# Graph attention, two graphs at a time: scores and contexts in one stretch, one transpose for both

## The chip, the cores and the metric

One core of a Trainium2 chip runs the whole program; there is one launch. The metric is the time of one execution in microseconds. Engines: TensorE (PE, with PEld for its weight loads), VectorE (DVE), ScalarE (ACT), GpSimd (POOL) and SyncE (SP), which issues the DMAs.

## The reference

For each of 128 graphs with 128 nodes and 384 features: layer norm, relu, attention with 6 heads of 64 masked by the graph's adjacency matrix, an output projection, and the input added back.

```python
h = jnp.maximum(_layernorm(x, axis=-1), 0.0)
q = _heads(h @ Wq + bq); k = _heads(h @ Wk + bk); v = _heads(h @ Wv + bv)
scores = jnp.einsum('bhqd,bhkd->bhqk', q, k) / np.sqrt(HEAD_SIZE)
probs = jax.nn.softmax(scores + jnp.where(adj, 0.0, NEG)[:, None], axis=-1)
ctx = jnp.einsum('bhqk,bhkd->bhqd', probs, v)      # heads side by side: 384
return x + ctx @ Wf + bf
```

Inputs: x (128, 128, 384) and four 384 x 384 weights with biases in float32, adj (128, 128, 128) bool. Everything is computed to about float32 accuracy.

## The kernel before

A float32 matmul is replaced by three float16 ones: each operand is split into an upper part (a rounded copy, made by ScalarE) and a lower part (the rest, made by VectorE or GpSimd), and `split_product` adds upper x upper, upper x lower and lower x upper in PSUM, nine matmuls per product.

The work is a software pipeline in slots of one graph. `slots` runs each engine's `slot(t, k)`: written out for the first slots, then in a loop of eight slots, then written out again. Each engine executes its list in the order in which `slot` calls its parts, and the semaphores (`wait`) tie the lists together. Nothing else sets the order. In slot t:

- SyncE loads x of graph t + 11, transposes h of graph t + 8 by DMA (`turn_h`), stores the output of graph t - 3 and transposes the probabilities of graph t - 1 by DMA (L285).
- GpSimd makes 1/std and the shift of graph t + 9 (`factors`, four small instructions), the mask of graph t + 1, the lower half of h (L795), x plus the output bias of graph t + 4 (L807) and normalises graph t's probabilities in two halves of three heads (L816).
- ScalarE rounds the probabilities of graph t - 1 (L494), applies the norm (L505) and rounds h (L515) of graph t + 9, takes six exponentials of graph t (L473), and rounds Q/K tiles, v and the context.
- VectorE adds the mask to the scores (L650, two instructions), takes maxima (L664), makes the lower probabilities of graph t - 1 (L699), statistics of graph t + 10, the residual of graph t - 3 (L615), reciprocals, and the lower halves of Q/K, context and v.
- TensorE: scores of graph t (`scores`), output projection of graph t - 3, a Q/K tile for a group of four graphs (512 columns; six tiles in four slots, so every other slot has two), the context of graph t - 2 (`context`), the v projection of graph t + 4.

`scores` and `context` are 18 small matmuls each, in pairs that use half of the array. Scores (ps_s) take two PSUM banks, Q/K two, the context (ps_c) and the output projection (ps_r) one each, v (ps_v) two: eight in all.

Of the kernel before, what the change touches and what calls it, by code (L numbers as in the profile page):

```python
# [6 lines left out]
F16 = mybir.dt.float16  # L7
# [12 lines left out]
TILES = 2 * PAIRS  # L20
RING = 2 * GROUP
# [4 lines left out]
LOAD, STATS, NORM, TURN, LATE = 11, 10, 9, 8, 3  # L26
XB = 4
# [3 lines left out]
FIRST, LOOP_END = 4, GRAPHS - 12  # L31


def graph_attention(nc, x, adj, Wq, bq, Wk, bk, Wv, bv, Wf, bf, out):
    ctx = ExitStack()
    with ctx:
# [8 lines left out]

# [24 lines left out]
        x_in = sb("x_in", [128, RING, FEAT])  # L70
        x_bias = sb("x_bias", [128, RING, FEAT])
        adj_in = sb("adj_in", [128, 2, GROUP, NODES], U8)
        mask = sb("mask", [128, 2, NODES])
        stats = sb("stats", [128, 2, 6])
        moments = sb("moments", [128, 2, 2])
        rstd = sb("rstd", [128, 2, 2])
        shift = sb("shift", [128, 2, 2])
        h = sb("h", [128, 2, FEAT])
        h_parts = sb("h_parts", [128, 2, 2, FEAT], F16)
        ht = sb("ht", [128, 2, 2 * KT, COLS], F16)  # L80

# [4 lines left out]
        v_hi = sb("v_hi", [128, 2, GROUP, FEAT], F16)  # L86
        v_lo = sb("v_lo", [128, 2, GROUP, FEAT], F16)
# [4 lines left out]
        parts = sb("parts", [128, 2, 2, HEADS * NODES], F16)  # L92
        pt = sb("pt", [128, 2, 2 * HEADS, NODES], F16)
        ct_hi = sb("ct_hi", [128, PAIRS, NODES], F16)
        ct_lo = sb("ct_lo", [128, PAIRS, NODES], F16)
# [27 lines left out]
        x_loaded = [sem(f"x_loaded{r}") for r in range(RING)]  # L123
        adj_loaded = [sem(f"adj_loaded{p}") for p in range(2)]
# [14 lines left out]
        mask_step = sem("mask_step")  # L139
# [18 lines left out]
        def valid(u):  # L158

            return not isinstance(u, int) or 0 <= u < GRAPHS  # L160

        def wait(eng, semaphore, value):

            if not isinstance(value, int) or value > 0:
                eng.wait_ge(semaphore, value)  # L165

        def slots(eng, slot, weights=lambda t: None):


# [3 lines left out]
            with eng.Fori(FIRST, LOOP_END - RING + 1, RING) as base:  # L173
                for i in range(RING):
                    slot(base + i, FIRST + i)
            for t in range(LOOP_END, GRAPHS + LATE):
                slot(t, t % RING)

        def turns(u, k, d):

            r = (k + d) % RING
            return 2 * (u - r) + 16

        def group_of(t, k):

            return (k % RING) // GROUP, k % GROUP

# [3 lines left out]
        PROJECTED = [[0, 1], [2], [3, 4], [5]]  # L191
        COUNT = [1, 1, 2, 1, 1, 2]

        def tile_count(t, j, tile):

            slot = next(i for i in range(GROUP) if tile in PROJECTED[i])
            return 2 * (t + GROUP) + 2 * (slot - j) + (1 if PROJECTED[slot][-1] != tile else 2)

        PAIR_COUNT = [2, 5, 8]
# [7 lines left out]

        @block.sync
        def _(sp):
# [3 lines left out]
            def weights(t):  # L213

                column = lambda b: b.rearrange("(k p) -> p k", p=128)
                if t == 1 - LOAD:
                    with nc.allow_non_contiguous_dma(reason="a bias vector, once"):
                        sp.dma_start(bv_col[:, :], column(bv)).then_inc(bv_loaded, 16)
                    load_weight("f", Wf)
                if t == 2 - LOAD:  # L220
                    load_weight("q", Wq)
                if t == 3 - LOAD:
                    load_weight("v", Wv)
                if t == 4 - LOAD:
                    load_x(3)
                    load_weight("k", Wk)
                    with nc.allow_non_contiguous_dma(reason="bias vectors, once"):
# [4 lines left out]
                    for u in range(4, RING):  # L232
                        load_x(u)
# [617 lines left out]
```

## Time and profile before

| | |
|---|---|
| median of 3 runs | 1001.98 us (1000.74 to 1003.02) |
| profiled execution, its own time | 1000.85 us |
| its span in the profile | 999.0 us |
| busy: TensorE | 948.1 us (95%) |
| busy: VectorE | 838.4 us (84%) |
| busy: ScalarE | 780.8 us (78%) |
| busy: GpSimd | 670.3 us (67%) |
| granted TensorE clock, mean | 0.991; 0.77 in the last 24 us |
| DMA | 130.86 MB, 60.4% of 16 engines |

Matmuls overlap, so TensorE's busy time is the union of overlapping spans; what a block of matmuls costs is read from the starts of successive blocks. On VectorE and ScalarE too, an instruction starts a little before the one ahead ends, if it waits for nothing. The profile's chain of waits that ended last runs mostly over GpSimd (41%) and issue (44%); it follows one of several nearly equal chains.

### The profile page before, as it was taken

The page shows a single profiled execution, that of the slowest core. Times are in us where ns is not written, and L with a number is a line of the kernel's source. Part 1 is how long each engine was busy: PE and PEld are TensorE (multiplying, and loading weights), DVE is VectorE, ACT ScalarE, POOL GpSimd, SP SyncE. Part 2 cuts the span into 40 slices and gives each one's busy share as a digit, 9 for nine tenths or more (in the row PEclk, how much of TensorE's full clock was granted, in tenths as well). Part 3 has the DMA queues.
Part 4 walks back from the last instruction along what each step waited for, and adds up shares of the span by engine and source line. Part 5 has one row for each costly group of instructions (what it writes and reads, how often), then busy time and mean ns, then how long its engine had stood idle before and what let it go on. Part 6 is the DMA issues. An engine that isn't in the chain of part 4 may idle for free.

```text
span 999.0 us, 28223 instructions
## 1 busy us (share of the span) xinstructions
PE 948.1 (95%) x8649; PEld 510.8 (51%) x8649; DVE 838.4 (84%) x1621; ACT 780.8 (78%) x2373; POOL 670.3 (67%) x1163
## 2 busy tenths in 40 slices
PE   1889999999999999999999999999999999999976
PEld 0445555555555555555555555555555555555543
DVE  4688888888888888898888888888889888888774
ACT  3687788888878888888888887888888888888663
POOL 4676677777776767767777677776776777777431
PEclk9999999999999999999999999999999999999997
DMA  7447656566566565655656656656565565666454
GB/s 199 75 90 152 123 126 141 127 139 147 130 135 136 129 140 130 148 133 126 141 127 141 145 130 133 138 129 139 132 148 133 124 143 128 140 146 121 92 94 90
DMA packets 359834, 130.86 MB, mean 131 GB/s; under 512 B 325376, under 2 KB 359808, under 8 KB 359808
## 3 DMA queue, kind: packets, MB, share of 16 engines
q1 hardware_dynamic: 359808, 130.54, 60.4%
q8 instruction: 13, 0.21, 0.1%
q14 instruction: 13, 0.11, 0.0%
HBM read 29.82 MB, written 25.17 MB: 55 GB/s over the span
## 4 chain that ended last, share of the span: by engine, by line
issue 44%; POOL 41%; PE 5%; ACT 2%; POOLq 2%; DVE 2%; DMA 2%; SPq 0%; DVEq 0%; ACTq 0%
POOL x_bias L807 13%; POOL s L816 11%; POOL rstd L775 7%; POOL mask L786 3%; POOL shift L778 2%; POOL rstd L770 2%; PE ps_qk L301 2%; POOL shift L772 2%; DMA pt<-parts 2%; POOL h_parts L795 1%; POOLq L165 1%; PE ps_v L301 1%; PE ps_r L301 1%; ACT s L473 1%; DVE s L650 1%
## 5 line engine op out<-in xcount | busy, mean ns | idle before, releaser
L473 ACT ACTIVATE s<-s,neg_max 128x128 f32<-128x128 f32 x768 | 297.7, 390 | 53.3 <-DVE neg_max L664 53.3
L816 POOL TENSOR_TENSOR s<-s,inv_sums 128x384 f32<-128x384 f32 x256 | 212.2, 829 | 132.7 <-DVE inv_sums L639 132.7
L795 POOL TENSOR_TENSOR h_parts<-h,h_parts 128x384 f16<-128x384 f32 x128 | 121.3, 948 | 146.1 <-ACT h_parts L515 146.1
L301 PE MATMUL ps_v<-w_hi_v,ht 128*128 128x384 f16 x768 | 209.4, 328 | 0.0
L301 PE MATMUL ps_qk<-ht,w_hi_q 128*128 128x512 f16 x576 | 172.5, 381 | 3.6 <-DVE w_lo_q L545 3.3
L301 PE MATMUL ps_qk<-ht,w_hi_k 128*128 128x512 f16 x576 | 171.3, 379 | 0.0
L807 POOL TENSOR_TENSOR x_bias<-x_in,out_bias 128x384 f32<-128x384 f32 x128 | 170.1, 1329 | 0.4
L494 ACT ACTIVATE parts<-s 128x768 f16<-128x768 f32 x128 | 107.3, 838 | 55.0 <-POOL s L816 55.0
L650 DVE SCALAR_TENSOR_TENSOR s<-ps_s,unscale,mask 128x384 f32<-128x384 f32 x256 | 145.2, 609 | 1.0
L473 ACT ACTIVATION_READ_ACCUMULATOR s<-s,neg_max 128x1 f32 x768 | 145.5, 189 | 0.0
L301 PE MATMUL ps_r<-w_hi_f,ct_hi 128*128 128x384 f16 x384 | 128.2, 334 | 14.3 <-DVE ct_lo L688 13.1
L699 DVE TENSOR_TENSOR parts<-s,parts 128x768 f16<-128x768 f32 x128 | 136.9, 1070 | 1.9 <-ACT parts L494 1.9
L664 DVE TENSOR_REDUCE neg_max<-s 128x6 f32<-128x768 f32 x128 | 122.0, 953 | 9.3
L301 PE MATMUL ps_r<-w_lo_f,ct_hi 128*128 128x384 f16 x384 | 127.0, 331 | 0.0
L301 PE MATMUL ps_r<-w_hi_f,ct_lo 128*128 128x384 f16 x384 | 126.8, 330 | 0.0
L301 PE MATMUL ps_v<-w_lo_v,ht 128*128 128x384 f16 x384 | 125.2, 326 | 0.0
L505 ACT ACTIVATE h<-x_in,shift,rstd 128x384 f32<-128x384 f32 x128 | 90.4, 706 | 42.1 <-POOL shift L778 39.9
L301 PE MATMUL ps_qk<-ht,w_lo_q 128*128 128x512 f16 x288 | 109.7, 381 | 0.0
L301 PE MATMUL ps_qk<-ht,w_lo_k 128*128 128x512 f16 x288 | 109.2, 379 | 0.0
L627 DVE SCALAR_TENSOR_TENSOR k_lo<-ps_qk,qk_bias,k_hi 128x512 f16<-128x512 f32 x96 | 71.2, 741 | 45.3 <-ACT k_hi L453 45.2
L301 PEld LDWEIGHTS ps_v<-w_hi_v,ht 128*128 128x128 f16 x768 | 74.8, 97 | 53.3
L405 PEld LDWEIGHTS ps_c<-pt,v_hi 128*64 128x64 f16 x1536 | 68.5, 110 | 64.6 <-issue 44.2
(77 smaller groups left out, 1806.6 us busy)
## 6 DMA issues: line engine op xcount, KB each, us to landing
x_in<-in_x SPq DMA_DIRECT2D x128, 192.0 KB, 2.9
out<-y SPq DMA_DIRECT2D x128, 192.0 KB, 2.1
ht<-h_parts SPq DMA_TRANSPOSE x128, 2.9
adj_in<-in_adj SPq DMA_DIRECT2D x32, 64.0 KB, 2.7
pt<-parts SPq DMA_TRANSPOSE x128, 3.7
w_raw_f<-in_L_gnn_Wf SPq DMA_DIRECT2D x1, 576.0 KB, 5.2
w_raw_q<-in_L_gnn_Wq SPq DMA_DIRECT2D x1, 576.0 KB, 6.2
w_raw_v<-in_L_gnn_Wv SPq DMA_DIRECT2D x1, 576.0 KB, 7.3
```

What stands on the lines that cost most here:

```text
L301: last = mm(psum, parts_a[a](i), parts_b[b](i), start=n == 0, stop=n == len(todo) - 1)
L473: last = activation(s[:, b, hd, :], s[:, b, hd, :], ACT.Exp, bias=neg_max[:, b, hd:hd + 1], accum_out=sums[:, b, hd:hd + 1])
L494: activation(parts[:, b, 0, :], s[:, b, :, :].rearrange("p h n -> p (h n)"), ACT.Copy).then_inc(parts_hi, 1)
L505: activation(h[:, r % 2, :], x_in[:, r, :], ACT.Relu, bias=shift[:, r % 2, 1:2], scale=rstd[:, r % 2, 1:2]).then_inc(h_ready, 1)
L627: nc.vector.scalar_tensor_tensor(out=lower, in0=ps_qk[tile % 2][:, :], scalar=qk_bias[:, which, pair:pair + 1], in1=upper, op0=ALU.add, op ...
L650: nc.vector.scalar_tensor_tensor(out=s[:, b, odd * PAIRS:(odd + 1) * PAIRS, :], in0=ps_s[:, odd, 0:PAIRS * NODES].rearrange("p (h n) -> p ...
L664: nc.vector.tensor_reduce(neg_max[:, b, :], s[:, b, :, :], AX.X, ALU.max, negate=True).then_inc(max_ready, 1)
L699: tt(parts[:, b, 1, :], s[:, b, :, :].rearrange("p h n -> p (h n)"), parts[:, b, 0, :], ALU.subtract).then_inc(parts_lo, 1)
L775: nc.gpsimd.tensor_tensor(rstd[:, b, 1:2], rstd[:, b, 0:1], minus_half[:, :], ALU.pow).then_inc(rstd_step, 1)
L795: nc.gpsimd.tensor_tensor(h_parts[:, b, 1, :], h[:, b, :], h_parts[:, b, 0, :], ALU.subtract).then_inc(h_lo_ready, 1)
L807: nc.gpsimd.tensor_tensor(x_bias[:, r, :], x_in[:, r, :], out_bias[:, :], ALU.add).then_inc(xb_ready, 1)
L816: nc.gpsimd.tensor_tensor(s[:, b, half, :], s[:, b, half, :], inv_sums[:, b, half].unsqueeze(2).to_broadcast([128, PAIRS, NODES]), ALU.mul ...
```

## The change

The slot becomes two graphs (a duo). There are 64 duos, pipeline distances count in duos, and the loop runs four slots per turn.

- TensorE (one slot): Q/K tile, Q/K tile, output projection of the first graph of duo t - 3, v of the first graph of duo t + 1, Q/K tile, v of the second, output projection of the second, scores of both graphs of duo t, contexts of both graphs of duo t - 2. Three Q/K tiles a slot, made two duos ahead.
- PSUM: ps_s takes four banks (two per graph). Contexts, v and output projections share the two banks of ps_m.
- `parts`, `pt`, `ct_hi`, `ct_lo` hold both graphs; `parts` and `pt` have two buffers of a duo. One DMA transpose turns the probabilities of a duo, another its h.
- s has one buffer for each graph of a duo. Masked scores are one instruction per graph (768 columns), normalising is one, reciprocals are one, lower context is one for both graphs, h is rounded for both graphs at once (768 columns), and so is its lower half and the bias addition.
- x is loaded a second time into x_res for the residual; the bias is added there in place.
- The weights are loaded in another order and prepared in other slots.

```diff
+DUOS = GRAPHS // 2
+RING = 4
...
-LOAD, STATS, NORM, TURN, LATE = 11, 10, 9, 8, 3
-XB = 4
+LOAD, STATS, NORM, TURN, AHEAD, VALUES = 7, 6, 5, 4, 2, 1
+CONTEXT, LATE = 2, 3
...
-        ps_s = ps("ps_s", [128, 2, 512])
+        ps_s = ps("ps_s", [128, 2, 2, 512])
         ps_qk = [ps(f"ps_qk{i}", [128, COLS]) for i in range(2)]
-        ps_c = ps("ps_c", [128, 512])
-        ps_r = ps("ps_r", [128, 512])
-        ps_v = [ps(f"ps_v{i}", [128, 512]) for i in range(2)]
+        ps_m = ps("ps_m", [128, 2, 512])
...
+                if valid(t):
+                    if not static or t >= FIRST:
+                        wait(sp, parts_lo, 2 * t - 2)
+                    sp.dma_start(x_res[:, k, :, :], x_rows[:, bass.ds(2 * t, 2), :]).then_inc(xr_loaded[k], 16)
...
+                if valid(t - 2):
...
+                    sp.dma_start_transpose(pt[:, k % 2, :, :, :].rearrange("p g a n -> p (g a) n"),
...
+                    for i in range(2):
+                        wait(sp, y_ready, 2 * u + 1 + i)
...
+                    else:
+                        wait(pe, y_ready, 2 * (t - LATE) + 1)
+                    at = slice(i * NODES, (i + 1) * NODES)
+                    split_product(ps_m[:, i, 0:FEAT],
...
+                    elif valid(t + VALUES):
+                        wait(pe, v_ready, 2 * (t + VALUES) + 1)
+                    split_product(ps_m[:, 1 - i, 0:FEAT], [lambda n: ct_hi[:, i, n, :], lambda n: ct_lo[:, i, n, :]],
...
                     wait(pe, turned[ku % 2], 8 * (u - ku % 2) + 16)
-                    wait(pe, v_ready, u + 1)
-                    wait(pe, ct_lo_ready, u)
+                    if i == 1:
+                        if valid(t + VALUES):
+                            wait(pe, v_ready, 2 * (t + VALUES) + 2)
...
+                    else:
+                        wait(pe, y_ready, 2 * (t - LATE) + 2)
...
-                scores(t, k)
-                projection(t - 3)
-                qk_tile(tiles[0])
-                context(t - 2, k - 2)
-                v_tile()
-                if two:
-                    qk_tile(tiles[1])
+                                last = mm(ps_m[rows, i, at], a[:, ku, i, f:f + HEAD],
+                                          pt[:, ku % 2, i, b + odd * PAIRS + pair, :], start=n == 0, stop=n == 2)
+                    if i == 0:
+                        last.then_inc(ct_ps, 1)
+                qk_tile(0)
+                qk_tile(1)
+                projection(0)
+                values(0)
+                qk_tile(2)
+                values(1)
+                projection(1)
+                scores(0)
+                scores(1)
+                context(1)
+                context(0)
...
-                if isinstance(t, int) and t < -GROUP:
-                    norm()
-                    upper_h()
-                else:
-                    upper_probs()
-                    norm()
-                    upper_h()
-                    exponentials(0)
-                    qk_tile(tiles[0])
-                    context()
-                    exponentials(1)
...
+                upper_context()
+                norm(0)
+                qk_upper(0)
+                upper_probs(1)
+                exponentials(0, 0)
+                qk_upper(1)
+                exponentials(0, 1)
+                v_upper(0)
+                exponentials(1, 0)
+                qk_upper(2)
+                v_upper(1)
+                upper_probs(0)
+                norm(1)
+                exponentials(1, 1)
+                upper_h()
...
+                    wait(dve, scores_ps, 2 * u + 1 + i)
+                    wait(dve, mask_ready, u + 1)
+                    wait(dve, parts_lo, 2 * u - 1 + i)
+                    nc.vector.scalar_tensor_tensor(
+                        out=s[:, i, :, :], in0=ps_s[:, i, :, 0:PAIRS * NODES], scalar=unscale[:, 0:1],
+                        in1=mask[:, i:i + 1, :].to_broadcast([128, HEADS, NODES]),
+                        op0=ALU.mult, op1=ALU.add).then_inc(masked, 1)
...
+                def lower_probs(i):
+                    u, b = t - (1, 2)[i], (k - (1, 2)[i]) % 2
+                    if not valid(u):
+                        return
+                    wait(dve, parts_hi, 2 * u + 1 + i)
+                    tt(parts[:, b, i, 1, :], s[:, i, :, :].rearrange("p h n -> p (h n)"), parts[:, b, i, 0, :],
                        ALU.subtract).then_inc(parts_lo, 1)
...
+                masked_scores(0)
+                lower_context()
+                maxima(0)
+                qk_lower(0)
+                lower_probs(1)
+                masked_scores(1)
+                maxima(1)
+                residual(0)
+                qk_lower(1)
+                spread()
+                lower_v(0)
+                spread_done()
+                reciprocals(0)
+                mean_and_variance()
+                qk_lower(2)
+                lower_v(1)
+                residual(1)
+                lower_probs(0)
+                reciprocals(1)
...
-                    wait(pool, h_ready, u + 1)
-                    wait(pool, y_ready, u - RING + 1)
-                    nc.gpsimd.tensor_tensor(x_bias[:, r, :], x_in[:, r, :], out_bias[:, :], ALU.add
+                    wait(pool, xr_loaded[r], 4 * (u - r) + 16)
+                    nc.gpsimd.tensor_tensor(x_res[:, r, :, :], x_res[:, r, :, :],
+                                            out_bias[:, :].unsqueeze(1).to_broadcast([128, 2, FEAT]), ALU.add
                                             ).then_inc(xb_ready, 1)
...
+                    wait(pool, inv_ready, 2 * u + 1 + i)
+                    nc.gpsimd.tensor_tensor(s[:, i, :, :], s[:, i, :, :],
+                                            inv_sums[:, i, :].unsqueeze(2).to_broadcast([128, HEADS, NODES]),
...
-                mask_of_next()
+                normalised(1)
                 lower_h()
                 biased_x()
+                wait_for_mask()
                 normalised(0)
-                normalised(1)
+                mask_of()
```

The order of instructions on GpSimd, in one place of the written-out start. s is the probabilities, x_res or x_bias is x plus the output bias, h_parts is the lower half of h. Before, the slots of two graphs:

```order
L770 TENSOR_TENSOR rstd<-moments,eps 128x1
L772 TENSOR_TENSOR shift<-moments,minus_one 128x1
L775 TENSOR_TENSOR rstd<-rstd,minus_half 128x1
L778 TENSOR_TENSOR shift<-shift,rstd 128x1
L786 TENSOR_SCALAR mask<-adj_in 128x128
L795 TENSOR_TENSOR h_parts<-h,h_parts 128x384
L807 TENSOR_TENSOR x_bias<-x_in,out_bias 128x384
L816 TENSOR_TENSOR s<-s,inv_sums 128x384 x2
```

That is one slot, and the next repeats it. After the change, one slot of two graphs:

```order
L722 TENSOR_TENSOR rstd<-moments,eps 128x2
L725 TENSOR_TENSOR shift<-moments,minus_one 128x2
L729 TENSOR_TENSOR rstd<-rstd,minus_half 128x2
L733 TENSOR_TENSOR shift<-shift,rstd 128x2
L772 TENSOR_TENSOR s<-s,inv_sums 128x768
L753 TENSOR_TENSOR h_parts<-h,h_parts 128x768
L763 TENSOR_TENSOR x_res<-x_res,out_bias 128x768
L772 TENSOR_TENSOR s<-s,inv_sums 128x768
L745 TENSOR_SCALAR mask<-adj_in 128x256
```

The second graph's normalising has moved between the factors and the lower half of h, the mask to the end.

VectorE, one slot before, from the masked scores (s) on:

```order
L650 SCALAR_TENSOR_TENSOR s<-ps_s,unscale,mask 128x384 x2
L664 TENSOR_REDUCE neg_max<-s 128x6
L699 TENSOR_TENSOR parts<-s,parts 128x768
L674 BN_STATS stats<-x_in 128x6
L615 SCALAR_TENSOR_TENSOR y<-ps_r,unscale,x_bias 128x384
L639 RECIPROCAL inv_sums<-sums 128x3
L627 SCALAR_TENSOR_TENSOR q_lo<-ps_qk,qk_bias,q_hi 128x512
L681 BN_AGGR moments<-stats 128x2
L688 TENSOR_TENSOR ct_lo<-ps_c,ct_hi 128x384
```

After, the first twelve of a slot's instructions:

```order
L615 SCALAR_TENSOR_TENSOR s<-ps_s,unscale,mask 128x768
L654 TENSOR_TENSOR ct_lo<-ps_m,ct_hi 128x768
L625 TENSOR_REDUCE neg_max<-s 128x6
L597 SCALAR_TENSOR_TENSOR q_lo<-ps_qk,qk_bias,q_hi 128x512
L662 TENSOR_TENSOR parts<-s,parts 128x768
L615 SCALAR_TENSOR_TENSOR s<-ps_s,unscale,mask 128x768
L625 TENSOR_REDUCE neg_max<-s 128x6
L586 SCALAR_TENSOR_TENSOR y<-ps_m,unscale,x_res 128x384
L597 SCALAR_TENSOR_TENSOR k_lo<-ps_qk,qk_bias,k_hi 128x512
L636 BN_STATS stats<-x_in 128x6 x2
L670 TENSOR_TENSOR v_lo<-ps_m,v_hi 128x384
L606 RECIPROCAL inv_sums<-sums 128x6
```

The lower probabilities (parts) in this piece are those of the second graph of the duo before; the masked scores of the second graph, which use the same s, stand right behind them. The reciprocal is the first graph's.

## Rows read from the trace of the kernel before

**Rows 1.** Busy us: stretch, PE, PEld, DVE, ACT, POOL; clock, DMA share, GB/s.
```profile
100.00:900.00 800.00, 792.42 (x7317) 428.21 (x7314) 697.08 (x1354) 653.90 (x2004) 566.87 (x974) 1.00 0.62 135
```

**Rows 2.** The residual's line (VectorE) between 100 and 900 us.
```profile
L615 DVE SCALAR_TENSOR_TENSOR y<-ps_r,unscale,x_bias x108: 593/598/604, 102.5 to 892.0; 128x384 f32<-128x384 f32 x108
```

**Rows 3.** Order of time, TensorE: start, us, engine, line, what.
```profile
945.82 0.23 PE L347 MATMUL ps_s<-k_hi,q_hi 64*128 64x128 f16 x2
...
946.44 0.34 PE L301 MATMUL ps_r<-w_hi_f,ct_hi 128*128 128x384 f16 x1
...
947.91 0.59 PE L301 MATMUL ps_qk<-ht,w_hi_q 128*128 128x512 f16 x2
...
949.95 0.25 PE L405 MATMUL ps_c<-pt,v_hi 128*64 128x128 f16 x2
...
950.58 0.34 PE L301 MATMUL ps_v<-w_hi_v,ht 128*128 128x384 f16 x1
```

**Rows 4.** Order of time, two stretches: VectorE and GpSimd side by side.
```profile
29.57 1.41 DVE L545 SCALAR_TENSOR_TENSOR w_lo_f<-w_raw_f,w_scale,w_hi_f 128x1152 f16<-128x1152 f32 x1
...
30.21 1.55 POOL L795 TENSOR_TENSOR h_parts<-h,h_parts 128x384 f16<-128x384 f32 x1 [1.84 <-ACT h_parts L515]
...
500.11 0.91 POOL L795 TENSOR_TENSOR h_parts<-h,h_parts 128x384 f16<-128x384 f32 x1 [1.15 <-ACT h_parts L515]
...
500.41 1.42 DVE L699 TENSOR_TENSOR parts<-s,parts 128x768 f16<-128x768 f32 x1
```

**Rows 5.** Lines of lower probabilities and bias addition: ns least, median, most.
```profile
L699 DVE TENSOR_TENSOR parts<-s,parts x82: 947/1036/1437, 300.4 to 898.9; 128x768 f16<-128x768 f32 x82
...
L807 POOL TENSOR_TENSOR x_bias<-x_in,out_bias x82: 991/1356/1722, 302.0 to 899.2; 128x384 f32<-128x384 f32 x82
```

**Rows 6.** Order of time, VectorE.
```profile
502.83 0.71 DVE L627 SCALAR_TENSOR_TENSOR k_lo<-ps_qk,qk_bias,k_hi 128x512 f16<-128x512 f32 x1
...
503.56 0.52 DVE L688 TENSOR_TENSOR ct_lo<-ps_c,ct_hi 128x384 f16<-128x384 f32 x1
...
504.30 0.56 DVE L707 TENSOR_TENSOR v_lo<-ps_v,v_hi 128x384 f16<-128x384 f32 x1
504.78 1.13 DVE L650 SCALAR_TENSOR_TENSOR s<-ps_s,unscale,mask 128x384 f32<-128x384 f32 x2
505.94 0.95 DVE L664 TENSOR_REDUCE neg_max<-s 128x6 f32<-128x768 f32 x1
...
507.68 0.55 DVE L674 BATCH_NORM_STATS2 stats<-x_in 128x6 f32<-128x384 f32 x1
```

**Rows 7.** Order of time, ScalarE.
```profile
507.46 0.39 ACT L473 ACTIVATE s<-s,neg_max 128x128 f32<-128x128 f32 x1
...
508.62 0.67 ACT L453 ACTIVATE q_hi<-ps_qk,qk_bias 128x512 f16<-128x512 f32 x1
509.19 0.47 ACT L484 ACTIVATE ct_hi<-ps_c 128x384 f16<-128x384 f32 x1
...
512.47 0.83 ACT L494 ACTIVATE parts<-s 128x768 f16<-128x768 f32 x1
513.29 0.71 ACT L505 ACTIVATE h<-x_in,shift,rstd 128x384 f32<-128x384 f32 x1
```

**Rows 8.** Order of time, the hand-off from ScalarE through VectorE to GpSimd.
```profile
946.40 0.19 ACT L473 ACTIVATION_READ_ACCUMULATOR s<-s,neg_max 128x1 f32 x1
...
946.88 0.83 POOL L816 TENSOR_TENSOR s<-s,inv_sums 128x384 f32<-128x384 f32 x1 [1.27 <-DVE inv_sums L639]
```

**Rows 9.** Transposes of the probabilities, last number: us from issue to landing.
```profile
pt<-parts SPq DMA_TRANSPOSE x128, 3.7
```

**Rows 10.** Order of time: TensorE's first projection and first scores.
```profile
27.05 1.03 PE L301 MATMUL ps_qk<-ht,w_hi_q 128*128 128x512 f16 x2 [3.27 <-DVE w_lo_q L545]
...
46.14 0.23 PE L347 MATMUL ps_s<-k_hi,q_hi 64*128 64x128 f16 x2
```

**Rows 11.** Order of time, GpSimd: a one-element instruction.
```profile
505.02 0.19 POOL L770 TENSOR_TENSOR rstd<-moments,eps 128x1 f32<-128x1 f32 x1
```

More of the change, by code:

```diff
@@ L174, in slots @@
                 for i in range(RING):
-                    slot(base + i, FIRST + i)
-            for t in range(LOOP_END, GRAPHS + LATE):
+                    slot(base + i, i)
+            for t in range(LOOP_END, DUOS + LATE):
                 slot(t, t % RING)
[L179 to L186, printed above, removed]
-        TILE = [(0, 0), (1, 0), (1, 1), (0, 1), (1, 2), (0, 2)]
[L191 to L199, printed above, removed]
+        TILE = [(0, 0), (1, 0), (1, 1), (0, 1), (1, 2), (0, 2)]
         x_rows = x.rearrange("g n f -> n g f")
@@ L323, in slot, with qk_tile @@
             def slot(t, k):
-                p, j = group_of(t, k)
-                tiles = PROJECTED[j]
-                two = len(tiles) == 2
-                done = t + GROUP
-                project = valid(done)
-                start = isinstance(t, int) and t == -GROUP
-                def scores(t, k):
+                static = isinstance(t, int)
+                def qk_tile(i):
+                    if not valid(t + AHEAD):
+                        return
+                    tile = 3 * (k % 2) + i
+                    wn, pair = "qk"[TILE[tile][0]], TILE[tile][1]
+                    group, at = 1 - k // 2, slice(pair * 128, (pair + 1) * 128)
+                    if k % 2 == 0 and i == 0:
+                        for b in range(2):
+                            wait(pe, h_turned[b], 8 * (t + AHEAD) + 16)
+                    if static and t == -AHEAD and i < 2:
+                        wait(pe, w_lo_ready, 1 + i)
+                    wait(pe, qk_out, 3 * (t + AHEAD) + i - 1)
+                    split_product(ps_qk[(k + i) % 2].rearrange("p (d n) -> p d n", d=2),
+                                  [lambda i: w_hi[wn][:, i, at], lambda i: w_lo[wn][:, i, at]],
+                                  [lambda i: ht[:, group, :, i, :], lambda i: ht[:, group, :, KT + i, :]], (qk_ps, 1))
@@ L362, in qk_tile @@
-                def qk_tile(tile):
-                    if not project:
-                        return
-                    wn, pair = "qk"[TILE[tile][0]], TILE[tile][1]
-                    at = slice(pair * 128, (pair + 1) * 128)
-                    if start:
-                        wait(pe, w_lo_ready, 1 + 2 * tile)
-                    if j == 0 and tile == tiles[0]:
-                        for b in range(2):
-                            wait(pe, h_turned[b], 8 * (done + 2) + 16)
-                    wait(pe, qk_out, 2 * done - ((2 if tile == tiles[0] else 0) if two else 1))
-                    split_product(ps_qk[tile % 2][:, :],
-                                  [lambda i: w_hi[wn][:, i, at], lambda i: w_lo[wn][:, i, at]],
-                                  [lambda i: ht[:, 1 - p, i, :], lambda i: ht[:, 1 - p, KT + i, :]],
-                                  (qk_ps, 1 if two else 2))
```

568 lines of the change are left out of this document (264 added, 304 removed).

## The prediction

> **What bounds the kernel now.** I read the busy time of a long middle stretch first. Between 100 and 900 us TensorE is busy 792.4 of 800 us at full granted clock, VectorE 697, ScalarE 654, GpSimd 567 [rows 1]. The reader should see that TensorE is the bound and VectorE has about an eighth of its time free. The period comes from the residual instruction, once per graph: 108 of them from 102.5 to 892.0 us, so 789.5 / 107 = 7.38 us a graph, 14.76 us for two [rows 2]. Next, the order of time on TensorE, for what a change between kinds of matmul costs. A projection of nine 384-column matmuls takes 947.91 - 946.44 = 1.47 us; a Q/K tile with the changeover behind it takes 949.95 - 947.91 = 2.04, of which I count 0.10 as changeover and 1.94 as tile; one graph's scores take 946.44 - 945.82 = 0.62, one graph's context 0.63 [rows 3]. Nine pairs of those small matmuls lie 0.057 us apart, 0.51 in all, so each small block pays 0.10 going in and 0.11 coming out. Two graphs: three tiles 5.82, four blocks of 1.47 are 5.88, four small blocks 4 x 0.725 = 2.90; sum 14.60. The other 0.16 of 14.76 is waiting.
>
> **The change part by part.**
> *TensorE.* The same matmuls, but scores and contexts of two graphs in one stretch: 0.10 + 4 x 0.51 + 0.10 (scores to contexts, taken equal to the other changeovers) + 0.11 = 2.35. That makes 5.82 + 5.88 + 2.35 = 14.05 us a slot of two graphs. If TensorE stayed the bound this would be 0.71 us a slot.
> *What must keep up.* The softmax of a slot is now a ring through four engines. Its mark, E, is the moment ScalarE has issued the last exponential of the second graph. From E two branches run.
> GpSimd's branch: the accumulator read ends 0.09 after E, and 0.29 later, with the reciprocal and two hand-offs between, GpSimd starts: E + 0.38 [rows 8]. It then normalises the second graph (768 columns; 384 take 0.83), takes the lower half of h (384 take 0.91) and adds the output bias to x_res (384 take 0.99 undisturbed) [rows 4, 5, 8]. A 768-column form is not in the trace. Bounds: twice the duration, or twice less a fixed part, for which I take the 0.19 us of a one-element GpSimd instruction [rows 11]; so 1.47 to 1.66, 1.63 to 1.82, 1.79 to 1.98. With 0.05 overlap at the two joints the bias addition starts at E + 3.4 to 3.8 and ends at E + 5.17 to 5.74. Its x_res was fetched a slot before, so it waits for nothing.
> VectorE's branch: ScalarE rounds h (768 columns, 0.82 to the next start, as the same copy of probabilities does) and both contexts (0.47 and 0.37 more, 0.84) [rows 7]. VectorE starts the lower context at E + 1.69: 0.88 (twice 0.44), the maxima 0.87, a Q/K lower half 0.63 [rows 6], where a following instruction starts 0.08 before the end of the one ahead. So the lower probabilities of the second graph arrive at E + 4.07, when the bias addition has run for 0.3 to 0.7 us.
> *What they do to each other.* Both read two tensors from SBUF. In the trace, lower h began at 500.11, lower probabilities at 500.41; the first took its usual 0.91, the second ended 0.81 after it and took 1.42 instead of 0.95. The other way, lower h issued at 30.21 beside a VectorE instruction that ran until 30.98 and took 1.55: 0.77 of waiting and its own 0.91 less the joint [rows 4]. The extremes are 947 and 1437 ns for lower probabilities, 991 and 1722 for the bias addition [rows 5]. Whoever comes second waits for the other's end. Before, 384-column GpSimd instructions cost VectorE at most 0.49 us; now a 768-column one stands in its way.
> The Trainium skill, page SBUF — State Buffer, section Who interferes with whom, says more than these rows: whichever of the two issues first holds the shared ports for the whole instruction, and the other is blocked and not slowed. By that rule the wait here is E + 4.07 to the end of the addition, 1.1 to 1.7 us; by the largest delay the rows show it would be 0.49. The trace agrees as far as its overlaps go, 0.6 and 0.8 us.
> *The sum of the ring.* I take blocking to the end, because both directions in [rows 4] fit it to 0.05 us. From the end of the addition: 0.81 to the end of the lower probabilities; 0.03 and masked scores of the second graph as one instruction 1.05 (the pair takes 1.13, one join less); 0.03 and maxima 0.87; residual 0.52 [rows 2]; Q/K lower half 0.63; two statistics 0.94; lower v 0.48 [rows 6]: 5.36. Then reciprocal and hand-off 0.25 (the 0.29 less 0.04 going in) [rows 8], normalising the first graph 1.47 to 1.66, 0.03, rounding it 0.82, second norm of h 0.61, three exponentials 1.16 [rows 7]: that is the next E. Low end 5.17 + 5.36 + 0.25 + 1.47 + 0.03 + 2.59 = 14.87; high end 5.74 + 5.36 + 0.25 + 1.66 + 0.03 + 2.59 = 15.63. I take the middle, 15.25, against 14.05 for TensorE and 14.76 before. Without the block the ring would be 4.07 + 0.95 + 4.55 + 0.25 + 1.5 + 2.62 = 13.95, hidden under TensorE.
> *Merged instructions.* One masked-score, one reciprocal and one lower-context instruction instead of two save joints of 0.08 each on VectorE; they are in the ring where they lie on it. Merged factor instructions on GpSimd (four for two graphs) fall between the first graph's normalising and E, ahead of a wait: nothing. Should they run over, up to 0.9 us of block by the first graph's lower probabilities, they still end about at E.
> *DMA.* x is fetched twice (64 more transfers of 384 KB), the DMA engines are 62% busy now [rows 1]: nothing. One transpose of probabilities per slot is issued once the lower probabilities of the second graph are through, about E + 6.2, and behind the h transpose and x_res on the same queue, about E + 7.0. Half of it lands in 3.7 us now [rows 9]; the whole between 3.7 and 7.4. Contexts then start at E + 11 to 14.4. TensorE needs 1.3 us more for both, and ScalarE asks for them at the next E + 0.82 = E + 16.1, so up to 7.8 us stays hidden.
> *Three buffers in two.* Values, projections and contexts share two PSUM tiles. The second projection waits for VectorE's lower v, E + 10.9; with scores and contexts it ends near E + 14.8, ahead of E + 16.1: hidden by 1.2 us. The second values wait for the residual about 0.7 us, the second projection about 0.6.
> *Ends.* First matmul at 27.05 now [rows 10]; then about 28.5, since the transpose of the second pair of graphs hangs on the statistics behind all four weights. First scores after nine tiles instead of six: 46.14 [rows 10] plus 5.8 plus 1.5 gives 53.5. Two young slots bring E to about 78 at slot 2. Slots 3 to 59 carry the full ring: 57. Slots 60 and 61 no longer normalise h, 13 each by TensorE's work less its lead; 62 to 64 have no Q/K or values, about 31 together. After the last E: normalise and round 2.7, lower part 1, transpose 5.5, contexts 1.3, their two halves 1.8, two projections at half pace (the mean granted clock of the last 24 us was 0.77) 5.9, residual and store 3.8: 22.
> Total span 78 + 57 x 15.25 + 26 + 31 + 22 = 1026; the profiled execution was 1.9 us longer than its span (1000.85 against 999.0), so 1028, and the median of the three runs (1001.98) is 1.1 above that execution: 1029.
>
> **The rivals.**
> *A, the order of arrival turns out the other way and TensorE binds.* The lower probabilities get in before the bias addition, which then waits, to nobody's cost. For it: the margin is only 0.3 to 0.7 us over a chain of five VectorE and ScalarE instructions. Against it: if TensorE is late the margin grows. It decides when VectorE arrives before E + 3.4. Period 14.1, total 78 + 57 x 14.1 + 79 + 3 = 964: faster.
> *B, the block costs no more than rows have shown (0.5 us).* Period 14.45, total 984. Against it: [rows 4]. The two kernels tie at a period of (1002 - 160) / 57 = 14.77, a block of about 0.8 us.
> *C, the merged transpose is late.* If it takes 8.5 us from issue to landing, the contexts come 0.7 us after ScalarE asks, every slot: about 1065. For it: it goes behind the h transpose and x_res. Against: 7.8 us are free.
> *D, the change doesn't do what it says:* the stretch saves nothing on TensorE, and TensorE binds as in A. Period 14.6, total 992. Against it: the price of each changeover stands in [rows 3]. If the ring binds, this would not show in the time.
>
> **How the numbers follow.** Forecast 0.60 (1006 to 1051 by the ends of the ring), A 0.22, B 0.07, C 0.09, D 0.02. Less than 0.2% either way, about 2 us, cannot be told from no change; I count D and 0.01 of the forecast's low end there, 0.03. Faster: A and B, 0.29. Slower: the rest of the forecast and C, 0.68. The range reaches down to 962, which takes in the upper half of A and all of B, and up to 1054; about 0.12 lies below and 0.08 above. The likeliest case's own range is 1006 to 1051.
>
> **What would show it.** Period of the residual pairs 15.25 us; TensorE busy near 14.0 of 15.25, 92% in the middle, with waits of the second values and the second projection for VectorE; scores and contexts of two graphs 2.35 us from first to next kind of matmul. Lower probabilities in two kinds: one near 0.95 to 1.4 us, the other 2.0 to 2.7, ending 0.8 after a bias addition of about 1.9 us that began before it. Normalising about 1.55 us. The probabilities' transpose landing 5 to 7 us after issue with little waiting for it. It is wrong if the second kind of lower probabilities is near 1 us, if the middle shows TensorE at 99% again, or if the contexts wait for the DMA in every slot.

## The result, and the profile after

The changed kernel takes 1019.62 us (median of 4 runs, 1016.67 to 1020.32) against 1002.5 (4 runs of before on the same chip, 1000.74 to 1003.62): ratio 1.0167, 95% interval 1.0141 to 1.0192, so 1.7% slower. The forecast was 1029 us, with 962 to 1054 as its range and 1006 to 1051 as the likeliest case's own.

The head of the page, with the chain that ended last, and the busy time of the middle stretch, which answers to [rows 1]:

```profile
span 1017.6 us, 25540 instructions
PE 931.7 (92%) x8649; PEld 517.6 (51%) x8649; DVE 846.0 (83%) x1301; ACT 759.0 (75%) x2245; POOL 557.5 (55%) x587
issue 32%; DVE 26%; ACT 15%; PE 12%; POOL 8%; DMA 4%; SPq 1%; POOLq 1%; DVEq 0%; ACTq 0%
```

```profile
100.00:900.00 800.00, 766.72 (x7187) 424.81 (x7185) 697.92 (x1072) 625.50 (x1870) 463.66 (x478) 1.00 0.69 160
```

TensorE was at 99% before and is at 96% now. The forecast had 92%; the busy time counts overlapping matmuls whose ends are modelled, so it shows less waiting than there is, and the waits are read from the starts of blocks below. No engine is full, and the chain runs through all four in turn, as it would in a ring. The next rows are the bias addition and VectorE's lower probabilities (duration min/median/max in ns, first and last start):

```profile
L763 POOL TENSOR_TENSOR x_res<-x_res,out_bias x50: 1808/1816/1832, 112.4 to 846.7; 128x768 f32<-128x768 f32 x50
L662 DVE TENSOR_TENSOR parts<-s,parts x101: 948/1446/2122, 98.2 to 847.2; 128x768 f16<-128x768 f32 x101
```

The period is (846.7 - 112.4) / 49 = 14.99 us for two graphs, against 14.76 in [rows 2]. The median of the lower probabilities tells nothing: they come in two kinds, half of them near 0.95 us and half from 1.9 to 2.1, as one slot shows (start, duration, engine; in brackets the idle time before it and its releaser):

```profile
498.60 0.83 ACT L481 ACTIVATE h_parts<-h 128x768 f16<-128x768 f32 x1
498.99 1.47 POOL L772 TENSOR_TENSOR s<-s,inv_sums 128x768 f32<-128x768 f32 x1 [0.23 <-DVE inv_sums L606]
500.42 1.65 POOL L753 TENSOR_TENSOR h_parts<-h,h_parts 128x768 f16<-128x768 f32 x1
502.03 1.82 POOL L763 TENSOR_TENSOR x_res<-x_res,out_bias 128x768 f32<-128x768 f32 x1
502.54 2.11 DVE L662 TENSOR_TENSOR parts<-s,parts 128x768 f16<-128x768 f32 x1
504.79 1.02 DVE L615 SCALAR_TENSOR_TENSOR s<-ps_s,unscale,mask 128x768 f32<-128x768 f32 x1
505.27 4.52 SPq L238 DMA_TRANSPOSE pt<-parts  x1
509.28 0.18 DVE L606 RECIPROCAL inv_sums<-sums 128x6 f32<-128x6 f32 x1
509.54 1.47 POOL L772 TENSOR_TENSOR s<-s,inv_sums 128x768 f32<-128x768 f32 x1 [5.69 <-DVE inv_sums L606]
511.12 0.84 ACT L460 ACTIVATE parts<-s 128x768 f16<-128x768 f32 x1 [1.58 <-POOL s L772]
512.00 0.96 DVE L662 TENSOR_TENSOR parts<-s,parts 128x768 f16<-128x768 f32 x1 [0.29 <-ACT parts L460]
513.62 0.83 ACT L481 ACTIVATE h_parts<-h 128x768 f16<-128x768 f32 x1
```

E, the mark, is where ScalarE is done with the last exponential of the second graph and starts rounding h: 498.60, and again 513.62. The bias addition ends at 503.85; the lower probabilities, issued at 502.54, end at 504.65, 0.80 later, as if they had begun when the addition ended. They are 1.16 us longer than the undisturbed 0.95. The Trainium skill's rule that the prediction cited (SBUF — State Buffer, Who interferes with whom: the second to issue is blocked, not slowed) is borne out by these rows. The last row but one shows the same instruction beside no large GpSimd work: 0.96.

What TensorE waits for in this slot, and its one stretch of small matmuls:

```profile
505.10 0.59 PE L266 MATMUL ps_qk<-ht,w_hi_q 128*128 128x512 f16 x2
507.38 0.34 PE L266 MATMUL ps_m<-w_hi_v,ht 128*128 128x384 f16 x1 [0.17 <-DVE y L586]
509.42 0.34 PE L266 MATMUL ps_m<-w_hi_f,ct_hi 128*128 128x384 f16 x1 [0.41 <-DVE v_lo L670]
510.99 0.23 PE L350 MATMUL ps_s<-k_hi,q_hi 64*128 64x128 f16 x2
512.10 0.25 PE L374 MATMUL ps_m<-pt,v_hi 128*64 128x128 f16 x2
513.26 0.60 PE L266 MATMUL ps_qk<-ht,w_hi_q 128*128 128x512 f16 x2
```

The second projection starts at 509.42 and takes its 1.47 us [rows 3], to 510.89; from there to the next Q/K tile at 513.26 are 2.37 us, 2.35 forecast. What the two waits cost is read from the starts, since an idle time in brackets begins only at the modelled end of the matmul before. The Q/K tile ahead of the second values, the first row, takes 1.94 us by the prediction's count, to 507.04, so the values start 0.34 us late. They take 1.47 us, to 508.85, so the projection starts 0.57 us late. Together that is 0.91 us of the slot.

The probabilities' transpose (issue in ns, then landing in us), which answers to [rows 9]:

```profile
L238 SPq DMA_TRANSPOSE pt<-parts x51: 4346/4464/4617, 100.9 to 850.0; - x51
DMA to landing us min/median/max: 5.9/6.1/8.0
```

### The profile page after: what moved, and what is told of

The parts are those of the page before. It is cut to its first block, busy times and chain, and to the rows that moved or that the text cites. A ratio compares the mean times of both kernels' runs of the same rounds, so it can differ in the third digit from the quotient of the medians.

```text
span 1017.6 us, 25540 instructions
## 1 busy us (share of the span) xinstructions
PE 931.7 (92%) x8649; PEld 517.6 (51%) x8649; DVE 846.0 (83%) x1301; ACT 759.0 (75%) x2245; POOL 557.5 (55%) x587
## 4 chain that ended last, share of the span: by engine, by line
issue 32%; DVE 26%; ACT 15%; PE 12%; POOL 8%; DMA 4%; SPq 1%; POOLq 1%; DVEq 0%; ACTq 0%
DVE parts L662 11%; POOL s L772 8%; DVE s L615 6%; PE ps_qk L266 5%; ACT s L440 5%; DVE neg_max L625 4%; PE ps_m L266 4%; ACT ct_hi L451 4%; ACT parts L460 3%; ACT h L470 3%; DMA pt<-parts 3%; DVE q_lo L597 2%; PE ps_m L374 1%; DVE ct_lo L654 1%; DMA w_raw_f<-in_L_gnn_Wf 1%
## 5 line engine op out<-in xcount | busy, mean ns | idle before, releaser
L772 POOL TENSOR_TENSOR s<-s,inv_sums 128x768 f32<-128x768 f32 x128 | 188.2, 1470 | 386.5 <-DVE inv_sums L606 386.5
L266 PE MATMUL ps_m<-w_hi_v,ht 128*128 128x384 f16 x768 | 208.7, 327 | 12.0 <-DVE y L586 12.0
L266 PE MATMUL ps_m<-w_hi_f,ct_hi 128*128 128x384 f16 x384 | 127.6, 332 | 30.6 <-DVE v_lo L670 21.1
L615 DVE SCALAR_TENSOR_TENSOR s<-ps_s,unscale,mask 128x768 f32<-128x768 f32 x128 | 130.2, 1017 | 15.8 <-issue 5.8
L266 PE MATMUL ps_m<-w_lo_f,ct_hi 128*128 128x384 f16 x384 | 126.8, 330 | 0.0
L266 PE MATMUL ps_m<-w_hi_f,ct_lo 128*128 128x384 f16 x384 | 126.8, 330 | 0.0
L266 PE MATMUL ps_m<-w_lo_v,ht 128*128 128x384 f16 x384 | 125.2, 326 | 0.0
L763 POOL TENSOR_TENSOR x_res<-x_res,out_bias 128x768 f32<-128x768 f32 x64 | 116.9, 1827 | 0.0
L753 POOL TENSOR_TENSOR h_parts<-h,h_parts 128x768 f16<-128x768 f32 x64 | 106.7, 1668 | 4.5 <-ACT h_parts L481 4.5
L586 DVE SCALAR_TENSOR_TENSOR y<-ps_m,unscale,x_res 128x384 f32<-128x384 f32 x128 | 78.4, 613 | 31.1 <-PE ps_m L266 31.1
```

What stands on the lines that cost most here:

```text
L266: last = mm(psum, parts_a[a](i), parts_b[b](i), start=n == 0, stop=n == len(todo) - 1)
L586: nc.vector.scalar_tensor_tensor(out=y[:, i, :], in0=ps_m[:, 1 - i, 0:FEAT], scalar=unscale[:, 1:2], in1=x_res[:, (k - LATE) % RING, i, :] ...
L615: nc.vector.scalar_tensor_tensor(out=s[:, i, :, :], in0=ps_s[:, i, :, 0:PAIRS * NODES], scalar=unscale[:, 0:1], in1=mask[:, i:i + 1, :].to ...
L753: nc.gpsimd.tensor_tensor(h_parts[:, b, 1, :], h[:, b, :, :, :].rearrange("p a g n -> p (a g n)"), h_parts[:, b, 0, :], ALU.subtract).then ...
L763: nc.gpsimd.tensor_tensor(x_res[:, r, :, :], x_res[:, r, :, :], out_bias[:, :].unsqueeze(1).to_broadcast([128, 2, FEAT]), ALU.add).then_in ...
L772: nc.gpsimd.tensor_tensor(s[:, i, :, :], s[:, i, :, :], inv_sums[:, i, :].unsqueeze(2).to_broadcast([128, HEADS, NODES]), ALU.mult).then_i ...
```

## The experiments

Theory R: the bias addition, 768 columns wide, stands in the way of the lower probabilities in every slot, and this closes the ring at 15 us while TensorE could run at 14.05. Rivals: the ring is too long without the block as well; or the transpose is late; or the joined stretch saves nothing.

**1. The block taken away, all work kept.** On GpSimd the addition waits until the lower probabilities of the second graph are through.

```
                     wait(pool, xr_loaded[r], 4 * (u - r) + 16)
+                    wait(pool, parts_lo, 2 * t - 2)
                     nc.gpsimd.tensor_tensor(x_res[...], x_res[...], out_bias..., ALU.add)
```

> The changed kernel; only the GpSimd bias addition (x_res) now waits until VectorE has made the second graph's lower probabilities. Theory (the addition holds the ports that the lower probabilities need, whole instruction, and the ring through VectorE and ScalarE sets the period): both kinds of lower probabilities near 0.95 to 1.0 us, the addition starts about 5.0 us after the mark E, the ring falls to 13.9 us and TensorE binds at 14.05 plus a little waiting, period 14.1 to 14.4, total 965 to 985 us: faster than both kernels. Rival (the long lower probabilities are a symptom, the chain through ScalarE and PSUM sharing is long by itself): period stays 15.0, total 1015 to 1024.

Measured: 969.95 us (966.85 to 973.2), ratio to before 0.9693 (0.9663 to 0.9723). One added wait turns 1.7% slower into 3.1% faster. The stretch 100 to 850, and the two instructions:

```profile
100.00:850.00 750.00, 748.04 (x7183) 433.07 (x7182) 651.22 (x1066) 626.40 (x1873) 453.71 (x478) 1.00 0.73 170
```

```profile
L662 DVE TENSOR_TENSOR parts<-s,parts x107: 947/957/961, 100.4 to 845.7; 128x768 f16<-128x768 f32 x107
L764 POOL TENSOR_TENSOR x_res<-x_res,out_bias x54: 1812/1819/1831, 101.4 to 846.8; 128x768 f32<-128x768 f32 x54
POOL x_res L764 <- DVE parts L662: 94.3, 54, 3.1
```

No lower probabilities are longer than 0.961 us. GpSimd waits 94.3 us in all (54 times) for VectorE, at no cost that shows. TensorE is at 99.7%, and the period is (846.8 - 101.4) / 53 = 14.06 us. That mean still takes in one slot of 15.4 us, which ends at 153.6. From 200 us on, the marks E (the starts of ScalarE's rounding of h) of the changed kernel and of this one are:

```profile
L481 ACT ACTIVATE h_parts<-h x43: 825/827/832, 213.9 to 843.3; 128x768 f16<-128x768 f32 x43
L481 ACT ACTIVATE h_parts<-h x46: 826/827/831, 209.9 to 840.9; 128x768 f16<-128x768 f32 x46
```

(843.3 - 213.9) / 42 = 14.99 us, and (840.9 - 209.9) / 45 = 14.02 us, against 14.05 in the prediction's sum for TensorE. So the block is the cause, and the ring without it is shorter than TensorE's work.

**2. The addition in two halves** of 384 columns, in the old place, so that the wait is at most half as long.

```
-                        wait(dve, xb_ready, u + 1)
+                        wait(dve, xb_ready, 2 * u + 2)
...
-                    nc.gpsimd.tensor_tensor(x_res[:, r, :, :], ..., ALU.add).then_inc(xb_ready, 1)
+                    for i in range(2):
+                        nc.gpsimd.tensor_tensor(x_res[:, r, i, :], x_res[:, r, i, :], out_bias[:, :], ALU.add
+                                                ).then_inc(xb_ready, 1)
```

> The changed kernel with the bias addition as two 384-column instructions, no new wait. Theory (the port is held per instruction): the lower probabilities arrive about 0.5 us into the first half (about 0.97 us), wait for its end and go before the second half: they take 1.3 to 1.5 us instead of 2.0 to 2.1, period 14.2 to 14.5, total 973 to 990. Rival 1 (GpSimd keeps the port across both halves, or the two share bandwidth by bytes): 2.0 to 2.1 us and 1015 to 1024 in all. Rival 2 (something else than the port): no change, 1015 to 1024, whatever the halves do.

Measured: 975.44 us (975.02 to 977.16), ratio 0.9741 (0.9725 to 0.9758). Three rows show who waits for whom:

```profile
510.02 2.68 POOL L764 TENSOR_TENSOR x_res<-x_res,out_bias 128x384 f32<-128x384 f32 x2
510.54 1.30 DVE L662 TENSOR_TENSOR parts<-s,parts 128x768 f16<-128x768 f32 x1
511.97 1.02 DVE L615 SCALAR_TENSOR_TENSOR s<-ps_s,unscale,mask 128x768 f32<-128x768 f32 x1
```

Each half takes about 1.0 us alone (median 1011 ns over 105 of them, longest 1732). The first would end at 511.0; VectorE's instruction then runs its 0.95 and ends at 511.84. GpSimd's second half is blocked meanwhile: 2.68 us for the pair, 0.66 more than 2 x 1.01. So the block passes at the border of an instruction, 0.35 us for VectorE in place of 1.16.

**3. The addition ahead of the lower half of h.**

```
                 normalised(1)
-                lower_h()
                 biased_x()
+                lower_h()
```

> The changed kernel with the GpSimd bias addition and the lower half of h exchanged in order. Theory (any GpSimd instruction that reads SBUF and stands at that place blocks): the lower half of h now starts about 3.6 us after E and ends at 5.2; the lower probabilities take 1.9 to 2.1 us; period 14.9 to 15.0, total 1010 to 1022. Rival (it is x_res, its second load of x or its DMA writes, that slows the lower probabilities): they take under 1.2 us, total under 990. The h transpose is issued 1.8 us later; if the DMA chain were near its limit, contexts would wait for it and the time would rise above 1030.

Measured: 1026.87 us (1026.06 to 1026.97), ratio 1.0257 (1.024 to 1.0274). That is between the two cases that were expected, and a partial miss: lower h, which now stands there, blocks the lower probabilities for less (they take 1310 ns in the mean of both kinds, 1515 in the changed kernel), yet the time is longer. One slot, with its mark E at 504.70 and the next at 519.72:

```profile
508.30 1.64 POOL L753 TENSOR_TENSOR h_parts<-h,h_parts 128x768 f16<-128x768 f32 x1
509.03 1.73 DVE L662 TENSOR_TENSOR parts<-s,parts 128x768 f16<-128x768 f32 x1
519.54 0.25 PE L374 MATMUL ps_m<-pt,v_hi 128*64 128x128 f16 x2 [1.16 <-DMA pt<-parts]
519.72 0.83 ACT L481 ACTIVATE h_parts<-h 128x768 f16<-128x768 f32 x1
```

VectorE issues the lower probabilities at E + 4.33, 0.39 later than in the changed kernel, and they end 0.82 us after lower h, at E + 6.06. In the changed kernel they ended at 504.65, E + 6.05. So the block is shorter only because VectorE comes later; the ring is not. The waits over 100 to 850 (total, times, longest) have a new one:

```profile
PE ps_m L374 <- DMA pt<-parts: 44.5, 49, 2.5
```

Contexts wait 0.9 us for the probabilities' transpose in every slot, once in 750 us in the changed kernel. Lower h ends 1.8 us later, so the h transpose, x_res and the probabilities' transpose behind it on the queue come later too, the last of them at E + 8.20 and not E + 6.67. But this wait does not set the period either. From 200 us on the marks are

```profile
L481 ACT ACTIVATE h_parts<-h x44: 825/827/829, 205.1 to 849.4; 128x768 f16<-128x768 f32 x44
```

which is (849.4 - 205.1) / 43 = 14.98 us, the changed kernel's period. What is lost lies almost all before: the mark of slot 8 is at 175.09 and in the changed kernel at 168.92, 6.2 of the 6.7 us by which the profiled spans differ (1024.3 against 1017.6). On the way there TensorE's contexts wait for the transpose once until 81.32, where they had started at 78.16 in the changed kernel, and once until 144.07, 1.1 us after a mark and so past the point at which ScalarE asks for them (E + 0.8):

```profile
81.32 0.32 PE L374 MATMUL ps_m<-pt,v_hi 128*64 128x128 f16 x2 [7.17 <-DMA pt<-parts]
144.07 0.32 PE L374 MATMUL ps_m<-pt,v_hi 128*64 128x128 f16 x2 [2.52 <-DMA pt<-parts]
```

The slots in which they fall take 19.1 and 17.2 us, against 16.3 and 15.0 in the changed kernel. So rival C's late transpose appears in every slot, brought about by an order that differs by one instruction, but it stays hidden behind the ring except in the run-in.

**4. The same order, the transpose in two,** the first graph's issued as soon as its lower probabilities are there.

```
+                if valid(t - 2):
+                    if static:
+                        wait(sp, parts_lo, 2 * t - 3)
+                    turn_probs(k, 0)
                 if valid(t + LOAD):       # x of the second graph
...
-                    sp.dma_start_transpose(pt[:, k % 2, :, :, :]..., parts[:, k % 2, :, :, :]...)
+                    turn_probs(k, 1)
...
-                    wait(pe, turned[ku % 2], 8 * (u - ku % 2) + 16)
+                    wait(pe, turned[ku % 2], 16 * (u - ku % 2) + 32)
...
-                    wait(act, turned[b], 8 * (u - b))
+                    wait(act, turned[b], 16 * (u - b))
```

`turn_probs(k, i)` is the DMA transpose of one graph's half, parts[:, k % 2, i] to pt[:, k % 2, i].

> The kernel with the bias addition ahead of the lower half of h (1026.9 us; its contexts waited for the probabilities' transpose in every slot), now with the transpose in two, the first graph's issued half a slot earlier. Theory (there the DMA chain h transpose, x_res, probabilities' transpose is what sets the period, and the ports no longer do): the contexts' wait goes, the period is that of the changed kernel less the shorter block of the lower probabilities (14.99 - 0.4 to 0.7 = 14.3 to 14.6), 985 to 1003 us. Rival (the port block sets the period in both orders and the wait for the transpose only shows it): 1015 to 1027 us, with TensorE waiting elsewhere.

Measured: 1017.11 us (1013.6 to 1019.84), ratio 1.0142 (1.0122 to 1.0162): the rival's case. The wait for the transpose is gone (0.5 us in 750, once), and the block is back in full:

```profile
506.43 1.64 POOL L760 TENSOR_TENSOR h_parts<-h,h_parts 128x768 f16<-128x768 f32 x1
506.76 2.11 DVE L669 TENSOR_TENSOR parts<-s,parts 128x768 f16<-128x768 f32 x1
```

```profile
L770 POOL TENSOR_TENSOR x_res<-x_res,out_bias x51: 1807/1818/1824, 100.1 to 849.4; 128x768 f32<-128x768 f32 x51
```

Lower h ends at 508.07, the lower probabilities at 508.87, 0.80 later. The period is (849.4 - 100.1) / 50 = 14.99 us, that of the changed kernel to 0.01. The same period stood in experiment 3. What was wrong in my expectation: I had taken the wait for the transpose for what set the period there, and the shorter block for a shorter ring. It does not matter which of GpSimd's two wide instructions is met; the last of the three ends at E + 5.25 in both orders (508.07 - 502.82 here, 503.85 - 498.60 in the changed kernel), and at E + 5.24 in experiment 3.

**5. One transpose or two, where TensorE binds:** experiment 1 with the edit of experiment 4.

> The kernel in which the bias addition waits for the lower probabilities, with the probabilities' transpose in two: the first graph's issued as soon as its lower probabilities are there, half a slot earlier, the second graph's at the old place. Theory (the joined transpose was hidden under TensorE, and joining it is worth nothing here): 967 to 973 us, as with one transpose, and the issue of 4.46 us falls to two of about 1.5. Rival (the joined transpose's late landing still costs something, or the second issue does): 3 us or more away from 970, below or above it.

Measured: 961.12 us (958.6 to 963.31), ratio 0.9601 (0.9586 to 0.9616), the fastest kernel here. I had expected 967 to 973; the rival was right, and most of it lies where I had not looked:

```profile
L771 POOL TENSOR_TENSOR x_res<-x_res,out_bias x54: 1812/1822/1826, 99.0 to 842.4; 128x768 f32<-128x768 f32 x54
```

Between the additions at 101.4 and 846.8 of experiment 1 and those at 99.0 and 842.4 here, the span differs by 2.0 us. Of the profiled spans' 10.1 us (966.9 against 956.8), 2.4 lie ahead of that and 5.7 behind it. From 200 us on the periods are equal: (837.2 - 206.1) / 45 = 14.02 us here, 14.02 in experiment 1.

```profile
L488 ACT ACTIVATE h_parts<-h x46: 826/828/831, 206.1 to 837.2; 128x768 f16<-128x768 f32 x46
```

Ahead of 200 us two slots differ by more than 0.3 us: the one whose mark is at 96.2 in experiment 1 and at 93.8 here takes 17.3 and 15.2 us, and the one whose mark is at 153.6 and at 149.9 takes 15.4 and 14.1. At the end, with few matmuls left, contexts wait for the joined transpose in the open: after 870 us TensorE's waits for it sum to 8.5 us in experiment 1 and 3.4 here (first row and second; total, times, longest):

```profile
PE ps_m L374 <- DMA pt<-parts: 8.5, 3, 4.7
```

```profile
PE ps_m L381 <- DMA pt<-parts: 3.4, 3, 1.5
```

Joining the transposes therefore costs time at the ends and in that one slot, and nothing in the steady middle.

**6. The stretch broken once,** on experiment 1: scores of the first graph ahead of the second projection.

```
-                projection(1)
                 scores(0)
+                projection(1)
                 scores(1)
```

> The kernel in which the bias addition waits for the lower probabilities (period 14.06 us, TensorE 99.7% busy), with scores of the first graph ahead of the second output projection instead of behind it, so that the stretch of small matmuls is broken once. Theory (each change between kinds of matmul costs TensorE 0.10 to 0.11 us, and TensorE binds there): one more pair of changeovers, 0.21 us a slot, period 14.27, about 970 + 60 x 0.21 = 982 us. Rival (the joined stretch saves nothing): 970 us, period 14.06. A third way: the first context waits for the residual of the second projection, which now ends half a microsecond before the contexts and not 1.1 us; then over 985 and the wait stands in TensorE's rows.

Measured: 982.25 us (979.37 to 985.46), ratio 0.9807 (0.9782 to 0.9831); 982 was expected. Between 200 and 850 us TensorE is busy for all of the 650.00 us, so the third way, a first context that waits for the residual, did not come about, and the rival (nothing saved, 970) falls. The marks from 200 us on give (837.4 - 211.2) / 44 = 14.23 us, 0.21 more than the 14.02 of experiment 1:

```profile
L481 ACT ACTIVATE h_parts<-h x45: 826/827/830, 211.2 to 837.4; 128x768 f16<-128x768 f32 x45
```

**7. The same wait in the kernel before,** ahead of its bias addition.

```
+                    if valid(t - 1):
+                        wait(pool, parts_lo, t)
```

> The kernel before; only its bias addition now waits until VectorE has made the lower probabilities of the slot. Theory (before, TensorE binds and VectorE has slack, so the same conflict cost nothing): additions all near 1.0 us, lower probabilities no longer than 1.44 us as before (the lower half of h still stands ahead of some), time 998 to 1005, the same as before within 0.3%. Rival (the port conflict costs the kernel before time too): more than 4 us faster.

Measured: 1002.07 us (10 runs, 1000.97 to 1003.65), ratio 1.0009 (0.9999 to 1.0018): no difference. The additions are all undisturbed now, and TensorE's busy time is 742.11 of 750 us, 742.77 without the wait:

```profile
L809 POOL TENSOR_TENSOR x_bias<-x_in,out_bias x102: 985/997/1011, 101.2 to 847.5; 128x384 f32<-128x384 f32 x102
```

But the edit frees GpSimd alone. VectorE's lower probabilities are as they were, since here it is the lower half of h that stands ahead of them (first row before, second with the wait, both over 100 to 850):

```profile
L699 DVE TENSOR_TENSOR parts<-s,parts x102: 946/958/1435, 101.1 to 846.4; 128x768 f16<-128x768 f32 x102
L699 DVE TENSOR_TENSOR parts<-s,parts x102: 947/958/1421, 100.0 to 845.8; 128x768 f16<-128x768 f32 x102
```

So it is shown that the additions' waits of up to 0.7 us cost nothing before. That VectorE's own waits of up to 0.49 us [rows 5] cost nothing either is argued, from TensorE's 99%, and no run took them away.

## Why the prediction was right

- *The bound moves from TensorE to the ring.* Right. TensorE waits for VectorE at the second values and the second projection, where I had said; by the starts of the blocks 0.34 and 0.57 us, against 0.7 and 0.6. The 0.91 us nearly fill the gap between its work and the period, 14.99 - 14.02 = 0.97.
- *TensorE's work.* 14.05 us: measured 14.02 where TensorE binds (experiment 1), and the stretch 2.37 against 2.35. Experiment 6 prices one pair of changeovers at 14.23 - 14.02 = 0.21 us a slot and 12.3 us in all; 0.21 was read from [rows 3]. Rival D falls.
- *Order of arrival.* GpSimd starts at E + 0.39 (0.38), the addition at E + 3.43 (3.4 to 3.8), the lower probabilities at E + 3.94 (4.07). Margin 0.51, within the 0.3 to 0.7. Rival A, whose time was 964, is what experiment 1 makes (970): it was the other outcome of half a microsecond, so a small miss in either branch would have turned the verdict round.
- *Blocked to the end.* Right: 0.80 from the addition's end to VectorE's, 0.81 from [rows 4]. The price is 1.16 us of VectorE's time, and 14.99 - 14.02 = 0.97 of period, where TensorE's work takes over as the bound. Rival B (0.5 us at most) falls with both numbers. That the block is a wait and not a slower pace shows in experiment 2 as well, where VectorE gets in at the border of the halves.
- *The size.* The term that was off is the duration of a 768-column GpSimd instruction. I took the middle between twice and twice less 0.19 us; measured are 1.47, 1.65 and 1.82, each within 0.03 of the low bound. The addition ends at E + 5.25 (5.17 to 5.74). The low end of the ring was 14.87; measured 14.99 against my 15.25, so 57 x 0.26 = 15 us too much.
- *The ends* took back some of it. By E of slots 2, 59, 61 and 64 (77.8, 931.3, 958.6, 994.9) the pieces are 77.8, 27.3, 36.3 and 22.7, 164 us in all; I had 78, 26, 31 and 22, 157. The miss is mostly slots 62 to 64. Contexts wait for the joined transpose in the open there, but that explains only part: with the transpose in two (experiment 4) the same three slots still take 997.55 - 962.81 = 34.7 us. What makes the rest was not taken apart. Slot 59, which I counted as full, took only 13.5 us (917.8 to 931.3).
- *DMA.* Landing 6.1 us (5 to 7 said). The prediction said nothing of the issue: it occupies the queue for 4.46 us. Its 7.8 us were the whole time from issue to landing that ScalarE leaves, so 1.7 were to spare. TensorE's own turn comes sooner, 0.7 us after the landing (505.27 + 6.1 = 511.4; contexts at 512.10). An issue 1.5 us later (experiment 3) uses up the shorter of these margins and not the longer: TensorE waits, and the period stays at 14.98. Rival C falls.
- *Two sums of the prediction are off by a little.* 0.7 us in each of 57 slots on top of 1029 is 1069, not the 1065 of rival C; the low end, 57 x 14.87 + 157 + 3, is 1008, not 1006. Neither changes the verdict.

Sum: 15 to 16 us too much in the middle, 7 too little at the ends, and 1 us more for what lies around the span than the median shows (1019.62 against a span of 1017.6) give the 9 us by which 1029 stands above 1019.62.

Not settled: the ring without the block is only known to be no longer than 14.02 us (experiments 1 and 5, where TensorE binds); my 13.95 was not measured. An estimate from the changed kernel is its period less the block, 14.99 - 1.16 = 13.83 us. Why one transpose costs 2 us in each of two single slots, one in the run-in and one near 150 us, was not taken apart.

## What to carry to other kernels

Fusing two small instructions into a wide one nearly doubles the time for which the other engine of such a pair can be shut out (the addition went from 0.99 to 1.82 us here), so look for the pair of two-input instructions of VectorE and GpSimd that meet, and ask on which of the two the ring hangs. If the one that comes first is not urgent, let it wait for the other: here one wait was worth 5%. A collision that costs nothing under one bound is a suspect once that bound is lowered. And a wait that a profile shows in every slot, like that for the transpose in experiment 3, need not be what sets the period: compare the periods before believing it.

## What the hardware showed that was not expected

- The joined transpose (128x3072 f16) occupies SyncE's queue for 4.46 us and lands in 6.1; the half-size one is issued in 1.43 us (507.06 in experiment 5) and lands in 4.5 there, 3.7 in [rows 9]. Twice the size took three times the issue.
- Even GpSimd's small pow on 128x2 is held up: 1.52 us beside the first graph's lower probabilities on VectorE, both started at 512.00, against 0.70 at 508.53 in experiment 6.

```profile
512.00 1.52 POOL L729 TENSOR_TENSOR rstd<-rstd,minus_half 128x2 f32<-128x2 f32 x1
```

```profile
508.53 0.70 POOL L729 TENSOR_TENSOR rstd<-rstd,minus_half 128x2 f32<-128x2 f32 x1
```

- Once in four slots, where the loop turns, VectorE stands 0.47 us ahead of its first instruction though nothing is awaited:

```profile
514.41 1.02 DVE L615 SCALAR_TENSOR_TENSOR s<-ps_s,unscale,mask 128x768 f32<-128x768 f32 x1 [0.47 <-issue]
```
